# Query and key products of the maximum pass cut to 64 rows by 32 queries

## The reference

```
x = x + 0.5 * ffn(layernorm(x))         # 512 -> 1024 -> 1024 -> 256, weights +1 or -1, relu twice
x = x + attention(layernorm(x))         # 16 heads of 16, causal, softmax over keys
x = x + 0.5 * ffn(layernorm(x))         # the same weights
scores = einsum('bhqd,bhkd->bhqk', q, k) / sqrt(16);  future keys masked
attn = softmax(scores);  ctx = attn @ v;  out = ctx @ w_o.T + b_o
```

## Time and profile before

| | us |
|---|---|
| median of 3 runs | 1571.55 (1568.6 to 1572.48) |
| the profiled execution | 1570.29 |
| its span in the profile | 1568.6 |
| TensorE matmul busy | 1539.0 (98%) |
| TensorE weight loads busy | 725.5 (46%) |
| VectorE busy | 1124.6 (72%) |
| ScalarE busy | 840.4 (54%) |
| GpSimd busy | 189.8 (12%) |

### The profile page before, as it was taken

The page is one execution under the profiler, slowest core; times in us unless marked ns, Lnnn a source line. Parts: engine busy times, 40 slices in busy tenths (PEclk is TensorE's granted clock), DMA queues, the critical chain, the costliest instruction groups (busy, mean ns, idle before and its releaser), DMA issues.

```text
span 1568.6 us, 35438 instructions
## 1 busy us (share of the span) xinstructions
PE 1539.0 (98%) x14112; PEld 725.5 (46%) x14112; DVE 1124.6 (72%) x1616; ACT 840.4 (54%) x1702; POOL 189.8 (12%) x514
## 2 busy tenths in 40 slices
PE   6999999999989999999999999999999999999998
PEld 3555555555433333343334333333333555555554
DVE  6535543554568999989988999998896667666552
ACT  3223322332148888888888888888886222222221
POOL 4300000000011122121122121112111000000000
PEclk9999999999989999999999999999999999999999
DMA  5122023202032222211222211222212221211210
GB/s 171 28 68 57 10 67 94 67 13 67 1 111 60 70 62 69 52 43 53 70 69 62 69 38 49 61 69 63 70 69 82 71 77 70 72 52 61 80 27 14
DMA packets 146227, 96.39 MB, mean 61 GB/s; under 512 B 106544, under 2 KB 125616, under 8 KB 146096
## 3 DMA queue, kind: packets, MB, share of 16 engines
q1 hardware_dynamic: 146096, 94.54, 21.6%
HBM read 49.15 MB, written 37.75 MB: 55 GB/s over the span
## 4 chain that ended last, share of the span: by engine, by line
PE 95%; DVE 2%; ACT 1%; SPq 1%; DMA 0%; issue 0%; DVEq 0%
PE ffn_mm L434 28%; PE ffn_mm L1266 18%; PE ffn_mm L1286 16%; PE ffn_mm L420 7%; PE ffn_acc L450 7%; PE ffn_acc L626 6%; PE ffn_tr L626 5%; PE ffn_mm L721 3%; PE ffn_acc L733 2%; PE ffn_acc L546 2%; DVE m_part L647 1%; PE ffn_tr L404 1%; ACT probs L1238 1%; PE ffn_tr L632 1%; PE ffn_acc L632 0%
## 5 line engine op out<-in xcount | busy, mean ns | idle before, releaser
L1238 ACT ACTIVATE probs<-ffn_mm 128x512 f32<-128x512 f32 (+3 forms) x1280 | 597.3, 545 | 122.1 <-PE ffn_mm L1266 116.3
L647 DVE TENSOR_REDUCE m_part<-ffn_acc 128x2 f32<-128x1024 f32 (+2 forms) x345 | 367.2, 1064 | 33.9 <-PE ffn_acc L626 29.1
L1266 PE MATMUL ffn_mm<-qk 128*32 128x512 f16 (+7 forms) x5120 | 387.9, 355 | 2.5 <-ACT probs L1238 1.8
L434 PE MATMUL ffn_mm<-ffn_h1h,w 128*128 128x512 f16 x1024 | 388.2, 379 | 0.0
L434 PE MATMUL ffn_mm<-ffn_h1l,w 128*128 128x512 f16 x1024 | 388.1, 379 | 0.0
L647 DVE TENSOR_REDUCE m_part<-ffn_tr 128x2 f32<-128x1024 f32 (+3 forms) x295 | 311.1, 1054 | 40.0 <-PE ffn_tr L626 24.7
L1286 PE MATMUL ffn_mm<-probs,v 128*32 128x512 f32 (+3 forms) x2560 | 305.5, 535 | 0.1
L500 ACT ACTIVATE ffn_h2h<-ffn_mm 128x512 f16<-128x512 f32 x128 | 76.4, 597 | 292.5 <-PE ffn_mm L434 291.1
L1266 PEld LDWEIGHTS ffn_mm<-qk 66*32 66x32 f16 (+1 forms) x5120 | 135.3, 94 | 210.2 <-ACT probs L1238 115.6
L511 DVE SCALAR_TENSOR_TENSOR ffn_h2l<-ffn_mm,ffn_h2h 128x512 f16<-128x512 f32 x128 | 85.7, 686 | 170.8 <-ACT ffn_h2h L500 170.8
L434 PEld LDWEIGHTS ffn_mm<-ffn_h1l,w 128*128 128x128 f16 x1024 | 100.2, 98 | 118.8
(11 more groups left out here) (114 smaller groups left out, 1031.2 us busy)
## 6 DMA issues: line engine op xcount, KB each, us to landing
qk<-qk_scr SPq DMA_DIRECT2D x256, 64.0 KB, 2.7
ctx_scr<-ctx_out SPq DMA_DIRECT2D x64, 256.0 KB, 2.7
qk<-ctx_scr SPq DMA_DIRECT2D x64, 256.0 KB
v_scr<-v_pad SPq DMA_DIRECT2D x32, 256.0 KB, 3.5
v<-v_scr SPq DMA_DIRECT2D x16, 512.0 KB, 4.6
x_res<-L_attn_x SPq DMA_DIRECT2D x8, 512.0 KB, 3.9
qk_scr<-qk_hi SPq DMA_DIRECT2D x32, 128.0 KB, 1.9
qk_scr<-qk_lo SPq DMA_DIRECT2D x32, 128.0 KB, 1.9
```

Source lines behind the costliest of these rows:

```text
L434: ins = nc.tensor.matmul(f.mm[:, m % 4, :], w1[:, kt, m * P:(m + 1) * P], part[:, kt, :], start=(kt == 0 and part is f.h1h), stop=(kt == H ...
L647: nc.vector.tensor_reduce(m_part[u][:, t, :, r], s_ps[slot][:, :, 0:w], AX.X, ALU.max).then_inc(sb.s_done, 1)
L1238: nc.scalar.activation(probs[:, g % P_SLOTS, j, c0:CH], st_ps[bank(k)][:, c0:CH], ACT.Exp, scale=scale_now).then_inc(se.exp_done, 1)
L1266: ins = nc.tensor.matmul(st_ps[bank(k)][c:c + 32, c0:CH], k_part(pair % 2, h, rows, slice(kb * P + c, kb * P + c + 32)), q_part(pair % 2, ...
```

## The change

Each head's matmul of a unit is cut into four of 32 queries, so that a unit has eight matmuls of 64 rows by 32 columns, with the tile position given by head (row 0 or 64) and query group (column 0, 32, 64, 96). The masks are cut in the same way; of their first half only the query groups 0 and 32 are issued, since `pick_row[:, 0, 64:]` is zero. Nothing else changes: the same products are summed, into the same banks, and the semaphore goes up with the last matmul of the unit.

```
                 for h in range(2):
-                    ins = nc.tensor.matmul(s_ps[slot][:, h, 0:w], q_part(u, h, HEAD_ROWS[h], slice(t * P, (t + 1) * P)),
-                                           k_part(u, h, HEAD_ROWS[h], slice(r * CH, r * CH + w)), start=True, stop=(r < i))
+                    for c in range(0, P, 32):
+                        ins = nc.tensor.matmul(s_ps[slot][c:c + 32, h, 0:w], q_part(u, h, HEAD_ROWS[h], slice(t * P + c, t * P + c + 32)),
+                                               k_part(u, h, HEAD_ROWS[h], slice(r * CH, r * CH + w)), start=True, stop=(r < i),
+                                               tile_position=(64 * h, c))
                 if r == i:
                     for hf in range(2):
+                        keys = slice(w - P + hf * 64, w - P + (hf + 1) * 64)
                         for h in range(2):
-                            keys = slice(w - P + hf * 64, w - P + (hf + 1) * 64)
-                            ins = nc.tensor.matmul(s_ps[slot][:, h, keys], pick_row[HEAD_ROWS[h], hf, :],
-                                                   mask_row[HEAD_ROWS[h], hf, :], start=False, stop=(hf == 1))
+                            for c in range(0, P if hf else 64, 32):
+                                ins = nc.tensor.matmul(s_ps[slot][c:c + 32, h, keys], pick_row[HEAD_ROWS[h], hf, c:c + 32],
+                                                       mask_row[HEAD_ROWS[h], hf, :], start=False, stop=(hf == 1),
+                                                       tile_position=(64 * h, c))
```

## The result

The changed kernel takes 1617.45 us (median of 4 runs, 1613.15 to 1623.23) against 1570.86 of before: a ratio of 1.0305, 95% interval 1.0282 to 1.0328 (these two medians alone give 1.0297). The forecast was slower, 1588.5, and the range ended at 1615. The sign holds. Of the mechanism a part holds: the costs of the tiles that I had forecast come to some 10 us. The larger part of the loss came by a path that I had put at 3.2 us, and 29 us are missing.

The account below looks back on a forecast made before the run. TensorE was taken to bound the kernel; stagger 10.8, masks 2.6, instruction issue 3.2 and early units 0.6 summed to 17.2 us more, so 1588.5 us, 1.1% slower, with a range of 1518 to 1615.

Parts of the forecast that it names:

- The bound: Stage of scores, products and maximum: TensorE is the bound, 46.1 us a pair of heads; VectorE is 9% idle.
- Changes of tile shape: Between units and scores or products: each change still costs about 0.10 us, 5.9 us a pair, so nothing is removed.
- Eight matmuls instead of two: In each unit: eight tiles stream together in 0.216 us as before; only the stagger grows, 10.8 us in all.
- The stagger: At the end of each run of units: last matmul starts later, 24 ns a run, 0.67 us a pair, 10.8 in all.
- the masks: Masks of 16 diagonal units a pair: extra stagger between rounds, some 10 ns each, 2.6 us in all.
- Issue: TensorE's sequencer: 20 ns per load and matmul against 46 available, mostly covered; 3.2 us for some diagonal units.
- no queue, DMA or wait moves: Outside TensorE's tiles: queues, DMA and waits stay as they were; no time was put down for them.
- Rival C: TensorE's instruction issue: bound at 59 ns for each load and matmul, 12.7 us more a pair, about 1775 us; chance 0.04.
- The sum: Whole kernel: stagger 10.8, masks 2.6, issue 3.2 and early units 0.6 add 17.2 us, giving 1588.5 us.

Follow-up runs that it names:

- e11: The kernel before, with units and masks cut as in the change but on 128 rows by 32 columns, using feed-forward weights: 1650.6 us, ratio 1.0502.
- e5: The changed kernel with 64 semaphore increments on TensorE's queue, once, ahead of the last feed-forward chunk: 1593.4 us, ratio 1.0146.
- e2: The changed kernel, loading only one of v's sixteen tiles from the third pair of heads on: 1590.1 us, ratio 1.0133.
- e9: The changed kernel without the semaphore increment in front of each unit: 1569.4 us, ratio 0.9996.
- e13: The changed kernel without those increments, but with small filler matmuls that restore TensorE's number of instructions: 1571.4 us, ratio 1.0014.
- e10: The kernel before without the semaphore increment in front of each unit: 1560.4 us, ratio 0.9936.
- e8: Units as 64 rows by 64 columns (masks 2 + 4), with 128 increments on TensorE's queue ahead of the last feed-forward chunk: 1597.7 us, ratio 1.0175.
- e1: The kernel before, each head's unit cut in four by keys, tile still 64*128, masks cut to 4 + 8: 1603.9 us, ratio 1.0223.
- e4: The changed kernel with units in four matmuls of 64 rows by 64 columns, masks 2 + 4: 1608.7 us, ratio 1.0242.

## Why the prediction was wrong

- *The bound.* Right: TensorE sets the pace of the stage, and between 600 and 700 us VectorE fell from 90.99 to 87.00.
- *Changes of tile shape.* Right: 0.33 to 0.34 us from start to start in both directions, and e11 shows that rows of another number are what costs it. The Trainium skill's "TensorEngine Tiling (Array Packing)", Tiling Modes, holds here: 64 by 32 beside 128 by 32 is another mode.
- *Eight matmuls instead of two.* Right that they stream together. The stagger was put at 24 ns a run, 0.67 us a pair. From a unit to the scores behind it the median rose from 0.320 to 0.339 us, 19 ns, so 0.53 over 28 runs; the whole pair rose by 46.74 - 46.11 = 0.63 (which also holds the masks, for which I had 0.16 more), and without increments by 0.35. No run has the stagger alone.
- *Issue.* This is the step that failed: the term of 3.2 us came to 34.6 in the stage. I took 10 ns for an instruction from one place and compared it with 46 ns for a load and its matmul, found the sequencer far ahead, and put down 3.2 us. Two things are missing in it. The first are the 41 increments of each pair, which I counted nowhere though they stand in the code ahead of each unit: 0.155 us each when they come in a row, so up to 6.4 us of a pair. The second is that instructions arrive by DMA, 256 at a time, while the next pair is loaded; a packet lasts 5.9 us here and lasted about 9 before (256 of 1317 in 46.1 us), so a late one is noticed sooner. In the kernel before packets started up to 14.1 us apart and no pause came of it. The pauses, 24.4 us, and the half clock behind them, 10.2 us, are this term. It needed all three: the changed number of instructions, fetches that fall into the loads (e5, e2), and the increments (e9, e13). So "no queue, DMA or wait moves" was wrong as well: the instruction queue moved 46 packets more.
- *Rival C.* It named the sequencer, but as a pace for all instructions (59 ns each, 1775 us). Nothing ran at such a pace: e9 issues its 996 pairs of instructions in 46.13 us. The Trainium skill's "TensorE: Matmul & The Clock Gate", section "Wait — 56ns, not 53.3ns?", gives the 62 ns for each MATMUL with hardware decode off; that isn't what bounds this program, since 996 would take over 61 us. The chance of 0.04 was for the wrong mechanism; a chance for single late packets was missing.
- *The sum.* 8.8 us for 14 pairs is 10 for 16, where I had 17.2. What is missing is pauses and half clock, 34.6 us, less this surplus of 7: 27 of the 29. (1571.55 + 17.2 is also 1588.8 and not 1588.5.) The direction came out as forecast, and e9 against e10, 9.0 us apart, shows that the tiles alone make the kernel slower too; so it wasn't luck, but the range was left by a mechanism that had no term in it.

The Trainium skill, "Runtime: NRT & Kernel Launch", section Instruction fetch mechanics, describes a refill in blocks of 16 KiB or 256 instructions, which the queue's packets show (11776 instructions, 46 packets), and calls the cost of crossing such a border mostly hidden. Here it wasn't: up to 2.3 us at a border.

What stays open: what an increment does inside the sequencer, so that without it no packet is late enough to be felt. That it keeps TensorE's queue from filling up is consistent with the waits of e9, but no run looked into the queue; nor does one tell the increment from the wait that stands on it. The trace shows when a packet moves, but not when it is asked for, so that the loads hold it up rests on e2 and e5 to e8. And why e1, with the changed kernel's count, its borders and its loads, pauses at four of these borders only, isn't shown.

## What to carry to other kernels

Cutting a matmul into more tiles that run together costs streaming time nothing and a few ns of stagger, but it multiplies instructions: count them for each period, with every semaphore instruction, against what the sequencer does in that time, and look at "issue" in the chain, not only at busy shares. If short pauses come once a period in the middle of an instruction group, count the instructions from one to the next. If it is a multiple of 256, look in the DMA view for the packet of the instruction queue ahead of each; when it lands just before the engine goes on, it came late, and a semaphore instruction or a burst of loads is the thing to try without. In this program a tile joined its neighbours without a gap only where rows and columns of the tile both agreed (operands of 66 rows beside 128 count as the same tile).

## What the runs showed of the hardware

- A semaphore increment on TensorE's queue took 0.155 us when they stood in a row (8.1, 18.0 and 27.9 us idle for 64, 128 and 192), where a weight load or a matmul took some 10 ns in one place.
- Taking one increment away ahead of each of 640 units, on which nobody waits, made the kernel before 0.64% faster (ratio 0.9936, 0.9920 to 0.9953), and is a version that beats both.
- Instructions arrive in packets of 256, and near a multiple of 256 to the period (2053 after, 1541 in e4, so 8 x 256 and 6 x 256 with five over) nearly the same instruction is at the border in pair after pair. It doesn't say how long the pauses are: e1 has 2053 as well and 7.0 us of them, the changed kernel 24.4, e13 none.
- In the changed kernel TensorE went on 1.2 to 1.5 us after a late packet had landed.
- A pause of 2.2 us was followed by some 3.4 us at 1.2 GHz, a loss of 1.7 us, nearly as much as the pause.
- Eight tiles of 64*32 with operands of their own ran together: 0.41 us from the first start to the last end, where two of 64*128 took 0.39.
